# An expert layer whose routed rows are scattered, weighted, to a table per token and choice, with half of the shared expert moved behind the routed tiles

## What is computed

```python
h = x + attention(rmsnorm(x, ln1_w), ...)
z = rmsnorm(h, ln2_w)
shared = silu(z @ sh_gate) * (z @ sh_up) / 8 @ sh_down            # 512 -> 256 -> 512
probs = sigmoid(z @ router_w + router_b)                          # 7 routed experts
scores, idx = top_k(probs, 2);  scores = scores / sum(scores)
combined = sum over e of w[e] * expert_ffn(z, r_gate[e], r_up[e], r_down[e])
ffn = h + shared + combined
out = x1 + layernorm(ffn)                                         # x1: the layer's own input
```

## Time and profile before

| what | us |
|---|---|
| median of three runs (2560.5 to 2569.09) | 2567.94 |
| the profiled execution's own time | 2555.55 |
| its span, first to last instruction | 2553.8 |
| busy PE / DVE / ACT / POOL in the span | 2198.5 / 1548.6 / 1042.2 / 990.9 |

### The profile page before, as it was taken

How to read it: one execution, slowest core, us unless ns; L and a number is a source line. 1 busy time by engine, 2 the same in 40 slices (tenths; PEclk the granted TensorE clock), 3 DMA queues, 4 the chain that set the end, 5 groups by cost and what they waited for, 6 DMA issues and landing times. The chain is left out here.

```text
span 2553.8 us, 38025 instructions
## 1 busy us (share of the span) xinstructions
PE 2198.5 (86%) x12992; PEld 1511.8 (59%) x12992; DVE 1548.6 (61%) x4168; ACT 1042.2 (41%) x2164; POOL 990.9 (39%) x1049
## 2 busy tenths in 40 slices
PE   6898899989889999898898988984998999999600
PEld 4665565666645656565565655642776788888500
DVE  3656766656567565666666666654564655655377
ACT  1435453334544333455433454542331455555300
POOL 1545634446464534555354455450433000000174
PEclk9999999999999999999999998986999999999855
DMA  5434554544535534354543443434455555555497
GB/s 172 113 110 125 146 161 116 141 117 116 142 110 159 155 108 116 100 150 143 155 130 102 114 128 100 108 83 141 167 203 203 194 183 211 191 200 204 155 325 251
DMA packets 228430, 386.11 MB, mean 151 GB/s; under 512 B 24718, under 2 KB 108558, under 8 KB 222606
## 3 DMA queue, kind: packets, MB, share of 16 engines
q1 hardware_dynamic: 157710, 290.87, 38.4%
q10 hardware_dynamic: 60288, 59.25, 6.8%
q0 software_dynamic: 10240, 33.56, 3.5%
HBM read 141.90 MB, written 140.51 MB: 111 GB/s over the span
## 5 line engine op out<-in xcount | busy, mean ns | idle before, releaser
L638 ACT ACTIVATE probs<-scoresT 128x512 f32<-128x512 f32 (+3 forms) x1024 | 417.3, 436 | 543.7 <-PE scoresT L1023 538.5
L819 DVE CUSTOM_DVE_ANT_0 unused<-score,mask 128x128 bf16<-128x128 f32 (+3 forms) x1024 | 465.6, 485 | 259.4 <-PE score L1000 245.5
L1000 PE MATMUL score<-stacks 96*128 96x256 f32 (+2 forms) x1024 | 388.0, 422 | 50.0 <-DVE rowmax L819 48.2
L1023 PE MATMUL scoresT<-stacks 97*128 97x256 f32 (+2 forms) x1024 | 404.5, 430 | 20.0 <-ACT probs L638 10.1
L571 POOL TENSOR_TENSOR probs<-probs 128x1536 f32<-128x1536 f32 (+1 forms) x128 | 372.8, 2913 | 45.9 <-PE out_ps L1037 38.0
L1000 PEld LDWEIGHTS score<-stacks 96*128 96x128 f32 x1024 | 180.0, 191 | 249.3 <-issue 178.5
L832 DVE RECIPROCAL total<-total 128x128 f32<-128x128 f32 x256 | 232.7, 932 | 96.5 <-ACT whole L649 91.2
L930 PE MATMUL middle<-wqkv,XT 128*128 128x128 f32 x2048 | 268.1, 278 | 7.0 <-ACT XT L605 6.1
L560 POOL TENSOR_SCALAR_AFFINE_SELECT probs<-probs 128x512 f32<-128x512 f32 x256 | 163.7, 640 | 281.7 <-ACT probs L638 281.5
L930 PEld LDWEIGHTS middle<-wqkv,XT 128*128 128x128 f32 x2048 | 258.4, 193 | 22.0 <-issue 8.4
L1023 PEld LDWEIGHTS scoresT<-stacks 97*128 97x128 f32 x1024 | 186.5, 192 | 123.6 <-ACT probs L638 71.4
(11 more groups left out here) (174 smaller groups left out, 3793.1 us busy)
## 6 DMA issues: line engine op xcount, KB each, us to landing
stacks<-parts SPq DMA_DIRECT2D x768, 128.0 KB, 2.5
x_slots<-mask ACTq DMA_DIRECT2D x56, 1024.0 KB, 4.8
xr<-x_slots SPq DMA_DIRECT2D x22, 1024.0 KB, 6.0
y_slots<-y SPq DMA_DIRECT2D x22, 1024.0 KB, 4.3
raw<-in_gates SPq DMA_DIRECT2D x23, 512.0 KB, 3.9
raw<-in_ups SPq DMA_DIRECT2D x23, 512.0 KB, 4.9
raw<-in_downs SPq DMA_DIRECT2D x23, 512.0 KB, 5.7
normed<-in_L_attn_x SPq DMA_DIRECT2D x8, 1024.0 KB, 8.6
```

Source lines behind the costliest of these rows:

```text
L638: act.activation(probs[j][:, h, 0:width], scoresT[:, u % ST_BANKS, first:first + width], ACT.Exp, scale=SCALE).then_inc(exp_done, 1)
L819: ins = dve.tensor_tensor_reduce(unused[:, t, 0:width], score.bank(name)[:, first:first + width], mask[:, T - width:T], 1.0, MASKED, ALU.a ...
L1000: ins = pe.matmul(score.bank(name)[:, first:first + width], heads[0:ROWMAX, 0, h, t * P:(t + 1) * P], heads[0:ROWMAX, 1, h, 0:width], star ...
L1023: pe.matmul(scoresT[:, u % ST_BANKS, 0:T - first], heads[0:ROWMAX + 1, 1, h, j * P:(j + 1) * P], heads[0:ROWMAX + 1, 0, h, first:T], start ...
```

## The change

Four things change, all in `expert_layer`.

1. The order of the steps is now written once, as a list (`expert_order`) that every engine walks through, each taking its own steps.
2. Only sequences 0 to 3 meet the shared expert first (**early** units 0 to 3); beside them all eight are opened, routed and scattered, two beside unit 0 (and the rest of sequence 0), two beside unit 1, three beside unit 2. Then come the 22 routed units, then sequences 4 to 7 with the shared expert (**late** units 26 to 29), whose scaled rows are kept in DRAM (`normed_kept`) and reloaded.
3. A row of `x_slots` has 516 columns in place of 512: the token's number, its first expert and its two weights go beside it. After a routed unit, ScalarE scales the result by the weight (`take_y`), VectorE works out where each row goes (`goals`, six operations on 4 columns), and GpSimd scatters it with 4 indirect DMAs to `y_rows`, one row per token and choice (`give`). `keep_y`, the gathers and `answers` are gone.
4. A closing loads its two blocks of `y_rows` whole (`load_pair`), GpSimd adds them (`add_pair`, 128x2048), VectorE adds the sum to h and shared, takes statistics (`close_stats`) and adds x1 (`close`); ScalarE normalizes. Closings m = 0 to 7 (order 4, 0, 5, 1, 6, 2, 7, 3) are written in pairs behind the units from 27 on: two at unit 27, two at 28, two at 29, two at the end.

Beside this, `rank` sums with 5 matmuls in place of 11 (each counted twice in rows), and the zeros written to `x_slots` during attention have runs of 344 columns in place of 256.

The core of the diff, first the order of steps: the early units, the routed ones, the closings.

```diff
                 def clear(k):
-                    CLEAR = T - 2 * P
+                    CLEAR = TT * ROW // 6
                     act.dma_start(x_slots[k:k + 1, :, :].rearrange("k p (j c) -> p (k j) c", c=CLEAR),
-                                  mask[:, 0:CLEAR].unsqueeze(1).to_broadcast([P, TT * D // CLEAR, CLEAR]))\
+                                  mask[:, 0:CLEAR].unsqueeze(1).to_broadcast([P, TT * ROW // CLEAR, CLEAR]))\
                        .then_inc(cleared, 16)
...
+def opened_sequences(blocks):
+    late = list(range(EARLY, blocks))
+    beside = [[late[u], u + 1] for u in range(EARLY - 1)]
+    beside[-1][1:1] = late[EARLY - 1:]
+    return beside
...
+    def closing_of(m):
+        if m + 1 < blocks:
+            yield "AY", m + 1
+        yield "CA", closing[m]
+        if m + PAIRS < blocks:
+            yield "LYY", m + PAIRS
+        if m > 0:
+            yield "CO", closing[m - 1]
+            yield "ST", m - 1
+            if m - 1 + XR < blocks:
+                yield "LX1", m - 1 + XR
+            if m - 1 + SUMS < blocks:
+                yield "LSM", m - 1 + SUMS
+        yield "CN", closing[m]
+    yield from [("LX", 0), ("LS",), ("LW", 0), ("LX", 1), ("LX", 2), ("LX", 3), ("LH", 0), ("LH", 1)]
+    yield from [("SQ", 0), ("NM", 0), ("WR",), *(("XT", 0, c) for c in range(CT)), ("SQ", 1), *(("SW", 0, k) for k in range(CHUNKS)),
...
+    nexts = iter([[("NM", 2), ("SQ", 3)], [("NM", 3), ("SQ", 4)], [("NM", 4), ("SQ", 5)], [("NM", 5), ("SQ", 6)],
+                  [("NM", 6), ("SQ", 7)], [("NM", 7)]])
+    opened = 1
+    for u in range(EARLY):
+        some = list(range(opened, opened + len(units.beside[u]))) if u + 1 < EARLY else [blocks]
+        opened += len(some)
+        first, second, third = (some + [None, None])[:3]
...
+        yield from splits(u, 0, 3)
+        yield "GU", u, 0, 1
+        yield "FA", u, 0
+        yield from columns(first, 2, 3)
+        yield "AH", u, 0
+        yield from splits(u, 3, CHUNKS)
+        if u == 0:
+            yield "RK", 0
+        yield from next(nexts, [])
+        yield "GU", u, 1, 0
+        yield from routed_too("LG", first)
+        yield "TA", u, 1
+        yield from columns(second, 0, 1)
+        yield from routed_too("ZT", first)
+        yield "GU", u, 1, 1
+        yield "FA", u, 1
+        yield from columns(second, 2)
+        yield "AH", u, 1
+        yield from columns(second, 3)
...
+        yield "FA", u, 0
+        if more:
+            yield "XT", o, 1
+        yield "AH", u, 0
+        yield from splits(u, 3, 5)
+        yield "GU", u, 1, 0
+        yield "TA", u, 1
+        if more:
+            yield "XT", o, 2
+        yield from splits(u, 5, 6)
+        yield "GU", u, 1, 1
+        yield "FA", u, 1
+        yield "AH", u, 1
+        if more:
+            yield "XT", o, 3
+        if more and units.kinds[u + 1][0] == "routed":
+            yield "EX", n + 1
+        if late > 0:
+            yield from closing_of(2 * late - 2)
+        yield "DN", u, 0
+        yield "DN", u, 1
+        if late > 0:
+            yield from closing_of(2 * late - 1)
```

SP's, GpSimd's and ScalarE's new steps:

```diff
+                def rows_free(o):
+                    b = o - XR
+                    if b >= 0:
+                        sp.wait_ge(*opening.full(("xT", b, CT - 1)))
+                    if 0 <= b < blocks:
+                        sp.wait_ge(scattered[b], 16 * TOP * TT)
+                        if sequences[b] >= EARLY:
+                            sp.wait_ge(xn_kept[sequences[b] - EARLY], 16)
+                    if blocks <= b < blocks + routed:
+                        sp.wait_ge(goal_done, b - blocks + 1)
...
+                def load_sums(m):
+                    s = closing[m]
+                    if m < 2:
+                        sp.wait_ge(h_kept, 16 * EARLY)
+                    elif m < SUMS:
+                        sp.wait_ge(*given((routed - 1) // GIVEN * GIVEN))
...
+                        sp.wait_ge(out_ready, TT * (m - SUMS + 1))
+                    source = summed if s < EARLY else h_in
+                    sp.dma_start(sums_of(m), source[s:s + 1, :, :].rearrange(rows, p=P)).then_inc(back_in[m % SUMS], 16)
...
+                def load_pair(m):
+                    s = closing[m]
+                    if m == 0:
+                        for k in range(routed - GIVEN, routed):
+                            sp.wait_ge(*given(k))
+                        sp.wait_ge(*opening.full(("z", max(o for o in range(blocks) if o not in units.unit_of))))
+                    if m >= PAIRS:
+                        sp.wait_ge(pair_added, m - PAIRS + 1)
+                        sp.wait_ge(pair_taken, TT * (m - PAIRS + 1))
+                    for j, to in enumerate(pair_of(m)):
+                        first = (j * blocks + s) * T
+                        sp.dma_start(to, y_rows[first:first + T, :].rearrange("(t p) c -> p t c", p=P))                          .then_inc(pair_in[m % PAIRS], 16)
+                def load_x1(m):
+                    s = closing[m]
+                    if m < XR:
+                        sp.wait_ge(*opening.full(("xT", blocks + routed + m, CT - 1)))
+                    else:
+                        sp.wait_ge(stored[m % XR], 16 * (m // XR))
+                    sp.dma_start(x1_of(m), x1_in[s:s + 1, :, :].rearrange(rows, p=P)).then_inc(x1_in_done[m % XR], 16)
+                def store(m):
+                    s = closing[m]
+                    sp.wait_ge(out_ready, TT * (m + 1))
+                    sp.dma_start(out[s:s + 1, :, :].rearrange(rows, p=P), x1_of(m)).then_inc(stored[m % XR], 16)
...
-                def bring(s):
-                    if s >= 2:
...
+                def give(k):
+                    pool.wait_ge(goal_done, k + 1)
+                    for t in range(TT):
+                        pool.wait_ge(y_done, TT * k + t + 1)
+                        pool.indirect_dma_start(
+                            out=y_rows, out_offset=bass.IndirectOffsetOnAxis(ap=goal[:, k % XR, t:t + 1], axis=0),
+                            in_=y[:, k % GIVEN, t, :], in_offset=None).then_inc(y_given[k % GIVEN], 16)
+                def add_pair(m):
+                    pool.wait_ge(pair_in[m % PAIRS], 32 * (m // PAIRS + 1))
+                    first, second = pair_of(m)
+                    pool.tensor_tensor(first, first, second, ALU.add).then_inc(pair_added, 1)
...
                 def take_y(u):
-                    k = u - blocks
-                    if k >= 2:
-                        act.wait_ge(y_kept[k % 2], 16 * (k // 2))
+                    k = units.kinds[u][1]
+                    if k >= GIVEN:
+                        act.wait_ge(*given(k - GIVEN))
+                    act.wait_ge(goal_done, k + 1)
                     for t in range(TT):
                         act.wait_ge(*down.full((u, t)))
-                        act.activation(y[:, k % 2, t, :], down.bank((u, t)), ACT.Copy).then_inc(y_done, 1)
+                        act.activation(y[:, k % GIVEN, t, :], down.bank((u, t)), ACT.Copy, scale=gain[:, k % XR, t:t + 1])\
```

VectorE's:

```diff
+                def close_stats(s):
+                    m = closing.index(s)
+                    dve.wait_ge(back_in[m % SUMS], 16 * (m // SUMS + 1))
+                    if s >= EARLY:
+                        u = units.kinds.index(("late", s))
                         for t in range(TT):
-                            if j > 0:
-                                dve.wait_ge(gained, TOP * TT * s + t + 1)
-                            dve.scalar_tensor_tensor(
-                                out=hsum[:, s % 2, t, :],
-                                in0=home[:, s % 2, 0:2, :].rearrange("p a n -> p (a n)").bitcast(F32)[:, t * D:(t + 1) * D],
-                                scalar=share[:, s, t, j:j + 1], in1=hsum[:, s % 2, t, :],
-                                op0=ALU.mult, op1=ALU.add).then_inc(gained, 1)
+                            dve.wait_ge(*down.full((u, t)))
+                            dve.tensor_tensor(sums_of(m)[:, t, :], down.bank((u, t)), sums_of(m)[:, t, :], ALU.add)\
+                               .then_inc(late_added, 1)
+                    dve.wait_ge(pair_added, m + 1)
                     for t in range(TT):
-                        dve.wait_ge(gained, TOP * TT * s + TT + t + 1)
-                        dve.bn_stats(stats[:, t, :], hsum[:, s % 2, t, :]).then_inc(stats_done, 1)
+                        if s >= EARLY:
+                            dve.wait_ge(late_added, TT * (s - EARLY) + t + 1)
+                        dve.tensor_tensor(sums_of(m)[:, t, :], pair_of(m)[0][:, t, :], sums_of(m)[:, t, :], ALU.add)                           .then_inc(pair_taken, 1)
                     for t in range(TT):
-                        dve.wait_ge(stats_done, TT * s + t + 1)
-                        dve.bn_aggr(meanvar[:, s % 2, t, :], stats[:, t, :]).then_inc(meanvar_done, 1)
+                        dve.wait_ge(pair_taken, TT * m + t + 1)
+                        if m > 0:
```

(15 more changed lines are left out.)

896 lines of the change are left out of this document (479 added, 417 removed).

## The result

The changed kernel takes 2537.0 us (median of 4 runs, 2536.0 to 2539.1), the kernel before 2568.5 beside it (4 runs, 2560.5 to 2569.1): a ratio of 0.9886, 95% interval 0.9865 to 0.9906, 31.5 us less. The forecast was 2521, with 2493 to 2545 as its range.

What follows compares the result with a forecast made beforehand. TensorE was taken to bound the routed units, DMA the tail. First tile 58 us earlier, 2 for an extra opening, 9 lost in the late phase: 47 us less, median 2521, 8 in 10 within 2493 to 2545.

Steps and rivals of the forecast that it cites:

- GpSimd in the late path: Rival, late phase: GpSimd's add, root and the lock in one queue; T+170 gives 2534, all of it 2553; chance 0.17.
- The base: Sum made against one profiled execution, span 2553.8, time 2555.6; the difference carried over to the median of 2567.9.
- Unit 0 starts at 1773: Start: unit 0 no longer waits for sequence 1's opening; 1773 against 1794.2, 21 us earlier.
- The early units end at 1902: Units 0 to 2: 98 us of TensorE work held up by scatters, reloads and squares, ending at 1818, 1857 and 1902.
- the clock costs 2 more: Early units: TensorE's reduced clock adds 2 us to 96, making 98.
- VectorE stands at the squares behind reload and scatter until 1813 and 1837: Units 0 and 1: squares wait for a reload that waits for a scatter, holding VectorE until 1813, then 1837.
- Nothing lost between the tile and the rhythm: After the first tile opens at 1924, 58 us earlier, units of 18.53 us follow with no wait.
- Routed units at no cost: Routed units: scatters, goals and scaling hide under TensorE's 18.53 us a unit; cost nothing.
- Late phase T+157: From late phase start T = 2350, a loop of closings ends at T+157, against 148 before: 9 us lost.
- closings fully covered: Rival, late phase: loads run ahead, bytes alone give T+140, or early VectorE waits halve; 17 us less, 2504; chance 0.22.
- Contention, 5 us: Late phase: GpSimd's adds block VectorE adds of two SBUF operands; 5 us taken, bounds 0 and 37.
- The two last rivals: Slower: closings one after another, 33 us each, 2662, chance 0.04. Nothing gained: routed units grow 2.1 us each, 0.03.

Runs made afterwards that it cites:

- c_before: The kernel before, unchanged, profiled a second time; 2567.24 us, one run.
- e_both: Changed kernel with the edits of e_lw and e_norm together; 2520.3 us, ratio to the kernel before 0.9832.
- e_sc: Changed kernel with the scatter of a unit's second opened sequence held behind the next unit's first row scale on GpSimd; 2542.7 us.
- e_sq: e_both plus VectorE's squares of the sequences opened fifth and sixth half a unit later; 2511.8 us, ratio to the kernel before 0.9802.
- e_lw: Changed kernel with SyncE issuing the weights of the unit after next before waiting for the sums of the unit just ended; 2535.8 us.
- e_norm: Changed kernel with ScalarE's normalisation of a closing one closing later in its order; 2533.0 us.
- e_row1: e_sq without loading each token's second row at the end (first added to itself), leaving out part of the computation; 2510.3 us.
- e_dve: Changed kernel with the two rows of each token added on VectorE instead of GpSimd; 2536.7 us.
- after: The changed kernel itself, profiled twice unchanged; median 2537.0 us, 2536.83 at the second profiling.
- e_half: Changed kernel scattering each token's row for its first choice alone, leaving out part of the computation; 2511.9 us.
- e_wide: The kernel before with rows of 516 numbers instead of 512 and nothing else of the change; 2564.1 us, one run.
- e_x1: e_sq with the load of x1 rows into a store's buffer one closing later, ahead of the next store; 2510.8 us.

## Why the prediction came out as it did

The sign, the mechanism and the range were right, the size was not: 47 us forecast, 31.5 measured, and the time lies above the likeliest case's own range of 2508 to 2535. It lies nearer the 2534 of the rival *GpSimd in the late path* than the forecast, but not for that rival's reason: the late phase took 160.1 us for its 170. Step by step, in the profiled executions (span forecast 2507, measured 2535.5: 28.5 us apart):

- *The base*, 5.3 of the 28.5. The attention part ended 5.3 us later than in the execution that the sum was made against (first load 1752.2 for 1746.9); c_before shows it at 1754.4 with no change at all. The forecast had added the 12 us by which that execution was below the median, which covered it, and more: of the 28.5 in the span 16 are left in the time.
- *Unit 0 starts at 1773*: 1777.3, that is 1772.0 on the forecast's base. Right.
- *The early units end at 1902*, on the measured base 1907.3: measured 1921.9. This is the step that failed, **by 14.6 us**, and in it above all the term "the clock costs 2 more". Unit 0 ended 2.5 earlier than forecast, unit 1 6.3 and unit 2 14.6 later. Two terms of it were mis-sized, and they overlap, so that their shares aren't a sum. TensorE's work was put at 98 us; it was busy 113.8, at a mean granted clock of 0.92, 0.86 and 0.90 (the windows above). The work itself was sized well: at the durations of the full clock (2.80 for 12 matmuls, 0.44 for four transposes, 1.28 for a rank) what the trace holds adds up to 99 us, an estimate. I had priced the half clock at 2 us, from one group after the wait for the tile. But by those means 31 us of these 145 are at the lower of the two levels (1.2 GHz), in part while TensorE is idle, and 46 of its 313 matmuls of 512 columns start 0.43 us after each other and not 0.23: about 9 us and not 2. From 1830 to 1850, during and behind the wait in unit 1, it is half the time. And the late completions, which nothing before showed: 7.5 us of the 145.4 by the difference to e_both, one execution each.
- *VectorE stands at the squares behind reload and scatter until 1813 and 1837*: the mechanism is shown, by e_sc, which made it longer, and by e_sq, which moved it away and won 7 us in unit 1. In the changed kernel itself it showed as 2.8 us in unit 0 and not at all in unit 1, where the late completions covered it: the squares ran from 1842.2 to 1844.7, and the forecast's 1837, their end, is 1842.3 on the measured base. Nearly the right number, for the wrong reason and so by luck; in unit 0 the wait was forecast at about 9 us and was 2.8. The profile alone doesn't tell the one cause from the other, the experiments do.
- *From the last unit to the tile*: 22 us forecast (1902 to 1924), 22.1 measured. The landing took 6.1 and not 4.5; the scatter started earlier by as much.
- *Nothing lost between the tile and the rhythm*: wrong by 5.5 us. The weights' order on SyncE was in the diff (`keep_h(3)` ahead of the third set of weights), and the prediction's walk through SyncE stopped at the tile. e_lw shows it and its price.
- *Routed units at no cost*: right, 18.53 us with no wait, GpSimd's scatters and the goals beneath them.
- *Late phase T+157*: 160.1, with a DMA share of 0.74 for the 0.85 forecast. The loop was forecast link by link and is there: unit 28's gate at T+58 for T+57, unit 29's at T+94 for T+91, the additions of a pair 4.6 us. e_norm shows that the link from the normalisation to the tanh binds, e_row1 that bytes alone don't (the rival *closings fully covered* took them for the bound).
- *Contention, 5 us*: the four groups of x1 additions that GpSimd's additions hit took 6.82, 4.92, 4.71 and 4.94 for 2.46, 11.6 us in sum; e_dve shows that it is GpSimd. In each group a single addition is held (5.04, 3.11, 2.90 and 3.13 us for 0.68), and each ends 0.55 us after GpSimd's. That is as the rule quoted from the Trainium skill ("SBUF — State Buffer", Who interferes with whom) has it, but only where the two meet: four times of eight and for 2.3 to 4.4 us, far from the 37 of its harshest reading. The 5 us that I added for it aren't what the first and longest meeting cost: it cost nothing in this order (under e_norm). So the loop without contention was put at T+152 and took up to 8 us more; for the three later meetings the cost isn't separated.

The two last rivals fell plainly: the closings came every 14.5 us in the mean (first store issued at 2428.5, last near 2530), not 33, and the routed units didn't grow.

What stays open is the cause of the late completions. They stand in five profiles of four kernels (after twice, e_lw, e_dve, e_norm) at the same instructions, in e_lw and e_norm at later ones too (unit 3's first group is recorded as ending at 1929.6 and 1925.9 and its tanh starts at 1939.1 and 1929.3), faintly in e_sc, and not in before, e_wide, e_half, e_both and e_sq; e_x1 and e_row1, with e_sq's early instructions, have single ones of 2.3 and 6.5 us. The same instructions run with and without them, so it isn't the order up to there; nor does the chip tell them apart: the record has chip 15 both for e_dve, which had them, and for e_both, which had not. Not tested is where the program's instructions lie, which differs between these kernels. One of e_dve's four runs took 2520.5 where the others took 2533.6 to 2539.9, so it may come and go with an execution; its trace wasn't taken. That halving the scatters removes them is therefore not shown.

## What to carry to other kernels

Where a change moves the point at which a phase begins, walk every in-order queue past that point, SyncE's for one more unit too: a wait for a unit's result placed in front of the next weights cost 5.5 us that no busy share showed. Price a stretch that waits often at the granted clock of such a stretch, not of the steady one. And take two profiles of the kernel before as the base of a sum; a step is best judged by the distance between two marks in the trace (unit to unit), since here the step worth 5.5 us was invisible in the kernel's time, the early units varying by up to 22 us between kernels with the same instructions there (137.9 in e_both, 159.9 in e_lw).

## What the runs showed of the hardware

Completions of TensorE reached the waiting engines 7.1 and 11.2 us after the recorded end of its matmuls, in one stretch of unit 1 (in e_lw in units 2 and 3 too), where 0.1 us is the rule; the chain names them "another core or an unknown queue" though the kernel runs on one core. TensorE's granted clock, 1.00 in the routed units, was 0.86 to 0.92 in the early ones, where it waits in every unit. A single VectorE subtraction of two SBUF operands took 4.08 us for 0.69 beside a GpSimd addition, and four VectorE additions so held each ended 0.55 us after GpSimd's instruction.
